# Graph attention, then three layers of a graph network: all eight transposes of a graph's probabilities in one row, the half projections behind them

## What is computed

```python
q = heads(x @ Wq); k = heads(x @ Wk); v = heads(x @ Wv)
scores = jnp.einsum('bhnd,bhmd->bhnm', q, k) / sqrt_dk
scores = jnp.where(mask, scores, -jnp.inf)
attn = jax.nn.softmax(scores, axis=-1)
out = jnp.einsum('bhnm,bhmd->bhnd', attn, v)
out = out.transpose(0, 2, 1, 3).reshape(b, n, d)
return jax.nn.relu(out) @ Wo
# then x = layernorm(x + ...), and x = layernorm(x + gnn(x, adj))
```

## Time and profile before

| | us |
|---|---|
| median of 3 runs (1639.92 to 1642.3) | 1641.13 |
| the profiled execution's own time | 1641.3 |
| its span, first to last instruction | 1639.5 |
| TensorE busy | 1611.0 (98%) |
| VectorE, ScalarE, GpSimd busy | 1320.2, 1232.7, 1327.4 |
| mean granted clock of TensorE | 0.996 |

### The profile page before, as it was taken

One profiled execution on the slowest core, in us unless ns is written; L12 is line 12 of the kernel. 1 busy time (PEld: TensorE's weight loads), 2 busy tenths in 40 slices (PEclk: granted clock), 3 DMA queues, 4 the chain that ended last, 5 costly groups with the idle time before them and its releaser, 6 DMA issues.

```text
span 1639.5 us, 40121 instructions
## 1 busy us (share of the span) xinstructions
PE 1611.0 (98%) x12036; PEld 1435.8 (88%) x12036; DVE 1320.2 (81%) x5321; ACT 1232.7 (75%) x2856; POOL 1327.4 (81%) x2367
## 2 busy tenths in 40 slices
PE   9999999978999999999999999999999999999997
PEld 8888888867898999989899898989989899898986
DVE  5999999987777777787877777777787888888875
ACT  7888898866777676777767776677777778787874
POOL 7788888856677787877878777787878999999996
PEclk9999999999999999999999999999999999999999
DMA  6334322212122121212213121121211222222211
GB/s 229 104 104 140 101 91 91 90 40 91 40 101 91 50 77 38 77 50 66 77 40 102 64 77 63 52 77 39 77 42 61 77 77 77 77 90 85 82 47 57
DMA packets 141721, 127.62 MB, mean 78 GB/s; under 512 B 12240, under 2 KB 132560, under 8 KB 141648
## 3 DMA queue, kind: packets, MB, share of 16 engines
q1 hardware_dynamic: 141648, 126.81, 24.2%
HBM read 89.04 MB, written 37.75 MB: 77 GB/s over the span
## 4 chain that ended last, share of the span: by engine, by line
PE 75%; DVE 1%; POOL 1%; ACT 0%; issue 0%; POOLq 0%; DVEq 0%; ACTq 0%
PE ps L45 33%; PE ps L979 32%; PE ps L951 5%; PE ps L965 3%; PE ps L943 1%; PE ps L958 1%; POOL n L169 0%; DVE gnn_junk L1111 0%; DVE xo L1222 0%; DVE res L1154 0%; POOL gnn_inv_last L913 0%; ACT gnn_w_hi L1067 0%; DVE gnn_st L1225 0%; DVE gnn_st L1178 0%; DVE gnn_st L1159 0%
## 5 line engine op out<-in xcount | busy, mean ns | idle before, releaser
L979 PE MATMUL ps<-gnn_w_hi,gnn_g_hi 128*128 128x256 f32 x1536 | 434.0, 283 | 1.5 <-DVE gnn_res L1174 1.5
L979 PE MATMUL ps<-gnn_w_lo,gnn_g_hi 128*128 128x256 f32 x1536 | 429.0, 279 | 0.0
L979 PE MATMUL ps<-gnn_w_hi,gnn_g_lo 128*128 128x256 f32 x1536 | 428.7, 279 | 0.0
L1079 ACT ACTIVATE gnn_g_hi<-ps,b_cols 128x512 fp32r<-128x512 f32 x384 | 264.4, 688 | 199.3 <-PE ps L45 199.3
L1182 DVE TENSOR_TENSOR gnn_g_lo<-ps,gnn_g_hi 128x512 fp32r<-128x512 f32 x384 | 262.8, 684 | 103.5 <-ACT ps L1080 103.4
L45 PE MATMUL ps<-gnn_hT_hi,gnn_w_hi 128*128 128x512 f32 x768 | 337.9, 440 | 0.0
L45 PE MATMUL ps<-gnn_hT_lo,gnn_w_hi 128*128 128x512 f32 x768 | 303.6, 395 | 0.0
L45 PE MATMUL ps<-gnn_hT_hi,gnn_w_lo 128*128 128x512 f32 x768 | 303.5, 395 | 0.0
L979 PEld LDWEIGHTS ps<-gnn_w_hi,gnn_g_hi 128*128 128x128 f32 x1536 | 288.7, 188 | 3.9 <-DVE gnn_res L1174 1.7
L979 PEld LDWEIGHTS ps<-gnn_w_lo,gnn_g_hi 128*128 128x128 f32 x1536 | 288.8, 188 | 2.3
L979 PEld LDWEIGHTS ps<-gnn_w_hi,gnn_g_lo 128*128 128x128 f32 x1536 | 288.7, 188 | 0.0
(11 more groups left out here) (145 smaller groups left out, 3994.4 us busy)
## 6 DMA issues: line engine op xcount, KB each, us to landing
x<-hist SPq DMA_DIRECT2D x49, 512.0 KB, 3.9
hist<-xo SPq DMA_DIRECT2D x48, 512.0 KB, 3.9
aw<-in_L_gnn_attn_w SPq DMA_DIRECT2D x48, 256.0 KB, 4.1
gmask<-mask_hist SPq DMA_DIRECT2D x48, 256.0 KB, 4.1
att_xT_raw<-in_xT SPq DMA_DIRECT2D x16, 512.0 KB, 3.3
att_xl<-in_x SPq DMA_DIRECT2D x16, 512.0 KB, 3.5
gnn_fin<-hist SPq DMA_DIRECT2D x15, 512.0 KB, 3.9
out<-gnn_fin SPq DMA_DIRECT2D x15, 512.0 KB, 3.0
```

Source lines behind the costliest of these rows:

```text
L979: mm = e.matmul(FF2[j % 2], g[a][:, m, j * N:(j + 1) * N], W2[b][:, m, :], start=(n == 0), stop=(n == len(terms) - 1))
L1079: e.activation(g[0][:, m, :], FF1[FFB[m]], ACT.Gelu, bias=bias)
```

## The change

In TensorE's body, the call of `fill` for slot 0 moves from between the two fours of transposes to behind the second four. The two waits in front of the second four stay with it. Nothing else is changed; every instruction remains.

```diff
                         for h in range(4, 8):
                             mm = e.transpose(PB[1][:, (h - 4) * N:(h - 3) * N], probs[j % 2][:, h, :], ident[:])
                         mm.then_inc(pT_made, 1)
-                        fill(t, par, j, 0, a1, a2)
                         e.wait_ge(exped, 2 * i + 2)
                         e.wait_ge(att_out, START + i)
                         for h in range(4):
                             mm = e.transpose(PB[0][:, h * N:(h + 1) * N], probs[j % 2][:, h, :], ident[:])
                         mm.then_inc(pT_made, 1)
+                        fill(t, par, j, 0, a1, a2)
                         fill(t, par, j, 1, a1, a2)
                         if j or before:
                             output_product(i - 1, has1)
```

## The result

The changed kernel takes 1645.42 us (median of 13 runs, 1644.42 to 1646.56), the kernel before 1641.54 us beside it (13 runs): ratio 1.0025, 95% interval 1.0016 to 1.0033. It is slower by 3.9 us, and 3.9 was the forecast (1645.1). The profiled executions took 1645.07 and 1641.3.

A forecast was written before the change was run, and what follows sets the result against it. TensorE, busy 98% of the span, was taken to bound the kernel. Own work -0.6, steady stalls +3.7 and the start +0.8 gave +3.9 us on 1641.2, so 1645.1 us, range 1641.0 to 1648.8.

The forecast's parts named there:

- TensorE's own work: TensorE's transposes and half projections in 59 attention bodies: nothing to -0.02 us each, -0.6 us taken.
- Steady stalls: Second fours in second and fourth graphs of each group wait for ScalarE's last exponentials: 2.1 + 1.6 = 3.7 us.
- The stall repeats: VectorE and ScalarE follow TensorE's output product, so each stall delays later inputs equally and is paid every time: 3.7 us.
- The start: Graphs 0, 1 and 3 at the stage's beginning lose 0.2, 0.2 and 0.4 us, together 0.8 us.
- The view that was to show it: TensorE's fours 0.53 apart where waiting, 0.44 elsewhere; some 27 waits for L526, none in first and third graphs.
- Absorbed stalls: Rival: VectorE and ScalarE don't slip with TensorE, so each kind of stall is paid once; 1641.5 us, chance 0.16.
- a cost of the row of eight, or of its clock: Clock rival: longer transpose rows pause TensorE's clock, 1.7 us per further slow stretch; 1647 us or more, chance 0.02.
- the free seam: Rival: the fifth transpose's weight load hides between the fours, 0.10 us per body, and stalls don't repeat; 1637, chance 0.06.
- stalls of the first and third graphs: Rival: later transposed reciprocals delay ScalarE, so these graphs stall too, +4.3 us on top; 1649.4 us, chance 0.13.
- the change did nothing: Rival: TensorE ran the weight loads in the old program's order; 1641 us, chance 0.03.
- The rule on transposes and the clock: Skill's rule that transposes don't engage TensorE's full clock: twice the row, twice the clock's pause; left out of the sum.
- The end of the stage: TensorE waits and its clock is at times down; where such stretches fall can shift, 1.7 us either way.

The follow-up runs named there:

- late copy, new order: Changed kernel, with ScalarE copying the projection bank behind the second half of the exponentials instead of in front: 1640.81 us against 1640.8, ratio 1.0001.
- the first eight graphs: Kernel before, with the second four moved ahead of the half projection in graphs 0 to 7 alone: 1641.77 us against 1640.8.
- the thirty free bodies: Kernel before, with the new order only in the first and third body of each group of four: 1640.84 us against 1640.8, ratio 1.0000.
- the late copy: Made alone: kernel before, old order, ScalarE copying the projection bank behind the second half of the exponentials: 1646.45 us against 1641.17, ratio 1.0032.

## Why the prediction was right, step by step

The mechanism was the forecast's. That the medians differ by 3.9 to the tenth is in part luck: TensorE's delay at graph 60 is 4.3, and in the profiled executions the end of the stage took most of the surplus back. The terms, against the 4.3:

- *TensorE's own work, -0.6.* Right: 0.010 per body where nothing waits (late copy, new order), some -0.6 for 59 bodies, though in first and second bodies alone. The weight load that is covered behind the first half projection comes uncovered between the fours.
- *Steady stalls, 3.7.* Right in place, size and number. The formula (distance of the last read less 0.33) gave 0.15 and 0.125; the distances of the fours are 0.54 and 0.51, as forecast from graph 59's 0.05. The period of four bodies grew by 0.27 where the terms give 0.15 + 0.13 - 0.04 = 0.24; over 13 groups (graph 4 to 56) this is the missing 0.4. It sits in the fourth bodies, which grew by 0.14 to 0.16; second ones mostly grew by 0.12 to 0.14 and first ones shrank by 0.02.
- *The stall repeats.* Right, and shown from two sides: a delay from the first eight graphs is still there 51 graphs on, and the loss in the second and fourth bodies goes on at the same rate to graph 59.
- *The start, 0.8.* Right in this trace, part by part: graphs 0 and 1 cost 0.21 and 0.22 (0.2 and 0.2 forecast), graph 3 costs 0.44 (0.4). But graph 3's part is not the same in every execution: it was 0.13 in that of the first eight graphs, so this term can be 0.3 smaller.
- *The view that was to show it.* Half wrong: I expected some 27 waits put down to L526. The list of TensorE's waits from 40 to 330 us has none and that of its weight loads ten. The distances were right, the list is too coarse for them.
- *Rivals.* Absorbed stalls are excluded by the first eight graphs; a cost of the row of eight, or of its clock, by the thirty free bodies; the free seam by the distance of 0.44; stalls of the first and third graphs did not occur: first graphs' reads stay at 0.00 relative to the first four, and third graphs' came even earlier (118.53 against 118.54, where it was 0.09 behind; 0.11 to 0.13 behind in graphs 34, 42 and 50, still below 0.33). The order of the rows (L469, L474, L45) excludes that the change did nothing.
- *The rule on transposes and the clock.* With eight transposes in a row the granted clock stays 1.00 from 160 to 330 us. The Trainium skill ("TensorE: Matmul & The Clock Gate", Part 4) says that the full clock does not engage for transposes; the price drawn from that for this change did not come. Other matmuls stand between the rows of eight, so this says nothing of longer runs of transposes.
- *The end of the stage.* In the two profiled executions it moved the difference by some 1.0 us (graph 62's body, above), within the prediction's 1.7 either way. Table of stretches of the changed kernel, as in the earlier trace rows:
```profile
160.00:330.00 170.00, 170.00 (x1901) 143.27 (x1894) 159.23 (x852) 150.23 (x615) 144.36 (x292) 1.00 0.30 94
350.00:358.00 8.00, 4.66 (x55) 3.21 (x53) 7.79 (x43) 5.14 (x23) 5.59 (x9) 1.00 0.32 99
...
366.00:380.00 14.00, 8.81 (x50) 7.16 (x49) 8.96 (x34) 6.71 (x12) 9.20 (x18) 0.88 0.36 113
```
The clock is down in another place than before (0.88 from 366 on, 1.00 where it was 0.79). Whether this also explains why the medians, over thirteen executions each, differ by 0.4 less than the delay at graph 60 is not shown.

## What to carry to other kernels

Work that stands between two uses of another engine's results is not idle packing: it is the slack of the second use. Before it is moved, compare the arrival of the late input with the new place, body by body, since a loop over four bodies can have two that arrive late. If the arrival hangs on the waiting engine's own output some bodies earlier, a stall of 0.15 us is paid every time; then either the producer's order must change with it (here the late copy, which makes the new order free, and costs 5.3 us if it is made alone), or the work stays between. Look for TensorE's short stalls in the distances of starts, since its idle time doesn't show them.

## What the runs showed that I had not expected

- A stall of TensorE of 0.15 us leaves no idle time in the profile, because the matmul before is drawn 0.27 long: 27 stalls, none in TensorE's own list, ten in that of the weight loads.
- A ScalarE copy behind the exponentials starts some 0.1 before the end of the last accumulator read (113.33 against 113.43), so the bank it frees is ready earlier than the read suggests: a stall of 0.17 instead of 0.27. The trace of the kernel before already had it (graph 17's read ends at 111.99, the next copy starts at 111.89).
- The place of the half projection has slack on both sides, used up by different engines: 0.7 us earlier and ScalarE's exponentials are late, 0.7 later and VectorE's copy is late, which from graph 4 on costs only where VectorE has an additional sum to do.
